# Attention of a fused graph block: values as weights in column groups instead of probabilities as weights

## The reference, cut to what matters

```
h = relu(layernorm(x))
q, k, v = split(h @ W_qkv)              # 4 heads of 32 features
s = q k^T / sqrt(32) + (adj == 0 ? -inf : 0)
x = x + softmax(s) v                    # the attention; the change is in this line
h = relu(layernorm(x))
h = relu(adj (h Wg0 + bg0));  h = relu(adj (h Wg1 + bg1))
for p in 1..4:                          # LSTMs over windows of p tokens
    h at the last token of each window = LSTM_p(window)
x = x + h
```

## Time and profile before

| | us |
|---|---|
| median of 3 runs | 554.71 (551.59 to 556.43) |
| the profiled execution | 551.66 |
| its span in the trace | 549.9 |
| PE busy | 503.4 (92%) |
| PE weight loads busy | 434.2 (79%) |
| DVE busy | 427.7 (78%) |
| ACT busy | 352.6 (64%) |
| POOL busy | 170.3 (31%) |
| mean granted clock of TensorE | 0.973 of full speed |

### The profile page before, as it was taken

The page is one execution under the profiler, slowest core; times in us unless marked ns, Lnnn a source line. Parts: engine busy times, 40 slices in busy tenths (PEclk is TensorE's granted clock), DMA queues, the critical chain, the costliest instruction groups (busy, mean ns, idle before and its releaser), DMA issues.

```text
span 549.9 us, 10009 instructions
## 1 busy us (share of the span) xinstructions
PE 503.4 (92%) x3464; PEld 434.2 (79%) x3464; DVE 427.7 (78%) x918; ACT 352.6 (64%) x573; POOL 170.3 (31%) x179
## 2 busy tenths in 40 slices
PE   3788999999999999999979999999999999999653
PEld 3577888888888888888867778889999888888533
DVE  3866787778877788776783788888888888788896
ACT  2445866668666686767757777777766577656241
POOL 2434424454344543541110012111121212233473
PEclk9999999999999999999998999999999999999975
DMA  7323000000000000000000000000000000000134
GB/s 216 102 81 92 2 2 1 2 0 0 0 0 0 0 0 0 0 0 1 2 1 0 2 0 1 1 0 2 1 1 1 2 0 1 0 1 20 58 95 134
DMA packets 18778, 11.29 MB, mean 21 GB/s; under 512 B 662, under 2 KB 17724, under 8 KB 18748
## 3 DMA queue, kind: packets, MB, share of 16 engines
q1 hardware_dynamic: 17052, 10.03, 6.3%
q10 hardware_dynamic: 1696, 0.87, 0.6%
HBM read 6.70 MB, written 4.19 MB: 20 GB/s over the span
## 4 chain that ended last, share of the span: by engine, by line
PE 62%; DVE 20%; ACT 8%; issue 6%; DMA 2%; POOL 1%; DVEq 0%; ACTq 0%; SPq 0%; POOLq 0%
PE ps L900 19%; PE ps L838 10%; PE ps L747 7%; PE ps L758 6%; DVE arena L1220 4%; DVE S_hi L1214 3%; PE ps L851 3%; DVE arena L1201 3%; PE ps L779 3%; PE ps L795 3%; PE ps L856 2%; ACT arena L587 2%; PE ps L942 2%; DVE arena L1191 2%; PE ps L769 2%
## 5 line engine op out<-in xcount | busy, mean ns | idle before, releaser
L601 ACT ACTIVATE arena<-ps,bias 128x512 f32<-128x512 f32 (+1 forms) x207 | 120.8, 626 | 38.3 <-PE ps L900 36.8
L565 ACT ACTIVATE arena<-ps 128x512 f32<-128x512 f32 (+1 forms) x112 | 85.5, 790 | 50.0 <-PE ps L758 42.3
L545 POOL TENSOR_TENSOR arena<-arena 128x512 f32<-128x512 f32 (+1 forms) x36 | 44.1, 1225 | 168.1 <-ACT arena L601 168.1
L900 PE MATMUL ps<-H_hi,W_hi 128*128 128x512 f32 (+2 forms) x207 | 76.0, 367 | 6.5 <-DVE S_lo L1216 5.1
L900 PE MATMUL ps<-H_lo,W_hi 128*128 128x512 f32 (+2 forms) x207 | 75.2, 363 | 0.0
L900 PE MATMUL ps<-H_hi,W_lo 128*128 128x512 f32 (+2 forms) x207 | 75.0, 362 | 0.0
L838 PEld LDWEIGHTS ps<-arena 128*128 128x128 f32 x512 | 64.1, 191 | 12.6 <-issue 8.4
L747 PE MATMUL ps<-ident,arena 128*128 128x128 f32 x384 | 54.6, 291 | 17.7 <-DVE arena L1220 7.8
L504 POOL TENSOR_TENSOR veps<-mv,eps 128x4 f32<-128x4 f32 x32 | 11.7, 365 | 187.0 <-DVE mv L1070 187.0
L838 PE MATMUL ps<-arena 128*128 128x33 f32 x512 | 63.5, 269 | 3.5 <-ACT arena L565 2.1
L747 PEld LDWEIGHTS ps<-ident,arena 128*128 128x128 f32 x384 | 46.1, 150 | 21.1 <-issue 9.3
(11 more groups left out here) (106 smaller groups left out, 1021.0 us busy)
## 6 DMA issues: line engine op xcount, KB each, us to landing
X<-in_x_dram SPq DMA_DIRECT2D x16, 256.0 KB, 2.8
out_dram<-X SPq DMA_DIRECT2D x14, 256.0 KB, 2.3
out_dram<-X ACTq DMA_DIRECT2D x2, 256.0 KB, 3.1
arena<-in_L_gnn_W_dram ACTq DMA_DIRECT2D x1, 128.0 KB, 3.0
wg<-in_L_gnn_Wg_dram ACTq DMA_DIRECT2D x2, 64.0 KB, 2.3
bg_rows<-in_L_gnn_bg_dram SPq DMA_DIRECT2D x6, 0.5 KB
wv<-in_L_gnn_W_dram ACTq DMA_DIRECT2D x1, 64.0 KB, 3.2
adj_sb<-in_adj_dram SPq DMA_DIRECT2D x1, 64.0 KB, 3.3
```

What stands on the lines that cost most here:

```text
L545: g_.tensor_tensor(ig[:, it.buf, 0:w], sig_i[:, it.buf, 0:w], tanh_g[:, it.buf, 0:w], ALU.mult)\
L565: a_.activation(to, psum, func).then_inc(ready, 1)
L601: a_.activation(to[:, it.buf, 0:w], ps[:, 4 * it.par + j, 0:w], func, bias=bias[:, col:col + 1])\
L900: l = mm(o, wt, v, start=m == 0, stop=m == len(terms) - 1)
```

## The change

The roles in the attention product are exchanged. The values (128 tokens x 32 features of one batch and head) become the weights, and the transposed probabilities (128 columns) move. Each head writes 32 partitions of the output, at partition 32h, so the four heads lie on four groups of 32 columns of the array. The output of a group is thus transposed: features on partitions, tokens on columns. The row sums come from four more products, with a 128x32 matrix of ones as weights and the 512 columns of each head moving; they stand in bank 5 beside the output in bank 4, repeated on the 32 partitions of the head, so that the division is elementwise. DVE takes the reciprocal of 128x512 sums and multiplies; PE transposes the quotient back into bank 5 (`attended`, four 128x128 transposes), and DVE adds it to `X` from there in the next iteration (`add_attention`, with the moments behind it).

The halves of the attention are gone: one `attend`, behind all masks, and one `over_sums`. PE's order in the iteration changes with it: K is projected behind `graph_mix`, `transpose_prob` half 1 stands behind `graph_linear_1`, `attended` stands between `scores` and the second `graph_mix`. DVE's `normalize` moves ahead of `shift` half 1. ACT's `hn2` and `u1T` move ahead of hT and gate 0. The memset of ones in `v_sb` on POOL goes.

```diff
-            def attend(s, half):
...
-                    for h in (2 * half, 2 * half + 1):
-                        o = b * 2 + h % 2
-                        l = mm(psO[:, half, o * (HD + 1):(o + 1) * (HD + 1)], probT[:, h, b * N:(b + 1) * N],
-                               v_sb[:, 1 - s.par, b, h, :], start=True, stop=True)
+            def attend(s):
+                pe.wait_ge(probT_ready, s.k * 2)
+                for h in range(HEADS):
+                    l = mm(psSum[h * HD:(h + 1) * HD, :], ones_f[:, 0:HD], probT[:, h, :], start=True, stop=True)
+                l.then_inc(att_sums, 1)
+                for b in range(GB):
+                    at_ = slice(b * N, (b + 1) * N)
+                    for h in range(HEADS):
+                        l = mm(psO[h * HD:(h + 1) * HD, at_], v_sb[:, 1 - s.par, b, h, :], probT[:, h, at_],
+                               start=True, stop=True)
+                l.then_inc(att_done, 1)
+
+            def attended(s):
+                pe.wait_ge(att_read, s.k)
+                transposed(psSum, batches(att)).then_inc(attT_done, 1)
...  (PE's iteration)
                 first_gate(s, 0, 0)
-                if s.mid:
-                    if s.front:
-                        pe.wait_ge(q_ready, k + 1)
-                    interleave([], attend(s, 0))
-                if s.front:
-                    if s.next1:
-                        pe.wait_ge(hT_hi_ready, k + 2)
-                    pe.wait_ge(att_read, 2 * k - 2)
-                    interleave([], project(s, psK, D, k_done))
                 pe.wait_ge(hn2_ready, k - 1)
...
                 interleave([], graph_mix(hn2, u1_done))
-                if s.mid:
-                    transpose_prob(s, 1)
+                if s.front:
+                    if s.next1:
+                        pe.wait_ge(hT_hi_ready, k + 2)
+                    pe.wait_ge(x2_ready, k - 1)
+                    interleave([], project(s, psK, D, k_done))
                 pe.wait_ge(u1T_ready, k - 1)
...
                 graph_linear_1().then_inc(z1_done, 1)
+                if s.mid:
+                    transpose_prob(s, 1)
                 first_gate(s, 1, 2)
...
+                    put_mask((2, 3))
+                    pe.wait_ge(q_ready, k + 1)
                     pe.wait_ge(k_ready, k + 1)
-                    masks = [lambda h=h: put_mask((h,)) for h in (2, 3)]
-                interleave(attend(s, 1), masks)
+                attend(s)
                 if s.front:
                     scores()
+                attended(s)
                 pe.wait_ge(h1_ready, k - 1)
...  (DVE)
-            def over_sums(s, half):
-                dve.wait_ge(att_done, s.k * 2 - 1 + half)
-                v_.reciprocal(rec4[:, half], o4[:, half, :, :, HD]).then_inc(rec_ready, 1)
...
+            def over_sums(s):
+                dve.wait_ge(att_sums, s.k)
+                v_.reciprocal(rec, psSum).then_inc(rec_ready, 1)
+                dve.wait_ge(rec_ready, s.k)
+                dve.wait_ge(att_done, s.k)
...
+                v_.tensor_tensor(att, psO, rec, ALU.mult).then_inc(att_read, 1)
+
+            def add_attention(k):
+                dve.wait_ge(attT_done, k - 1)
+                xg = X[:, ds(k * GB - 2 * GB, GB), :]
+                v_.tensor_tensor(xg, xg, psSum.rearrange("p (b d) -> p b d", b=GB), ALU.add).then_inc(x2_ready, 1)
+                dve.wait_ge(x2_ready, k - 1)
+                moments(1, k - 2, stats2, var2)
...  (DVE's iteration)
                 if s.back:
-                    dve.wait_ge(x2_ready, 2 * k - 2)
-                    moments(1, k - 2, stats2, var2)
+                    add_attention(k)
...
                 if s.finish:
                     output_lo(k - 3)
+                if s.back:
+                    normalize(1, k - 2, xn2, rstd2, xn2_ready)
                 if s.mid:
                     shift(s, 1)
...
-                if s.back:
-                    normalize(1, k - 2, xn2, rstd2, xn2_ready)
...
-                if s.mid:
-                    over_sums(s, 0)
...
                 if s.mid:
-                    over_sums(s, 1)
+                    over_sums(s)
...  (ACT's iteration)
+                read(hn2, hn2, xn2_ready, k - 1, hn2_ready, ACT.Relu)
                 if s.next1:
                     read_hT(psX[s.back], k + 2, 1 - s.par)
+                read(u1T[:], psA, u1_done, k - 1, u1T_ready)
                 if s.finish:
...
                     first_gate(k - 3, 0, act_i, 0, 0.5)
-                read(hn2, hn2, xn2_ready, k - 1, hn2_ready, ACT.Relu)
                 if s.mid:
                     exp(s, 1)
...
-                read(u1T[:], psA, u1_done, k - 1, u1T_ready)
```

More of the change, by code:

```diff
@@ L254, in gnn_block @@
         qT, kT, att = take(GT), take(GT), take(GT)
-        v_sb = take(V).rearrange("p (s b h d) -> p s b h d", s=2, b=GB, h=HEADS)
+        v_sb = take(2 * GT).rearrange("p (s b h d) -> p s b h d", s=2, b=GB, h=HEADS)
         prob = take(HEADS * GT)
@@ L258, in gnn_block @@
         probT = take(HEADS * GT).rearrange("p (h n) -> p h n", h=HEADS)
+        rec = take(GT)
         at[0] = attention_end = 16 * GT
@@ L296, in gnn_block @@
         psX = {True: psK, False: psB}
-        psO = ps[:, 4:6, :]
+        psO, psSum = ps[:, 4, :], ps[:, 5, :]
         def psW(m):
@@ L353, in gnn_block @@
         att_done = sem("att_done")
+        att_sums = sem("att_sums")
         rec_ready = sem("rec_ready")
         att_read = sem("att_read")
+        attT_done = sem("attT_done")
         x2_ready = sem("x2_ready")
@@ L492, in _ @@
             g_.memset(eps[:], LN_EPS)
-            g_.memset(ident[:], 0.0)
-            g_.memset(v_sb[:, :, :, :, HD:HD + 1], 1.0).then_inc(pool_chain, 1)
+            g_.memset(ident[:], 0.0).then_inc(pool_chain, 1)
             pool.wait_ge(pool_chain, 1)
@@ L654, in read_v @@
                 if s.back:
-                    act.wait_ge(att_done, 2 * s.k - 2)
-                a_.activation(v_sb[:, s.par, :, :, 0:HD], psA.rearrange("p (b h d) -> p b h d", b=GB, h=HEADS),
+                    act.wait_ge(att_done, s.k - 1)
+                a_.activation(v_sb[:, s.par, :, :, :], psA.rearrange("p (b h d) -> p b h d", b=GB, h=HEADS),
                               ACT.Copy).then_inc(v_ready, 1)
@@ L978, in fill @@
                     pe.wait_ge(w_lo_done, 2)
+                if s.mid:
+                    pe.wait_ge(probT_ready, k * 2 - 1)
                 put_mask((0, 1))
@@ L982, in fill @@
                     pe.wait_ge(k_ready, k + 1)
-                    interleave(attend(s, 1), [lambda h=h: put_mask((h,)) for h in (2, 3)])
+                    put_mask((2, 3))
+                    attend(s)
                 else:
@@ L1001, in iteration @@
                         pe.wait_ge(w_lo_done, 2 * MAX_SKIP)
-                    pe.wait_ge(att_read, 2 * k - 3)
+                    pe.wait_ge(att_read, k - 1)
                     interleave([], project(s, psQ, 0, q_done))
@@ L1036, in iteration @@
                 graph_linear_1().then_inc(z1_done, 1)
+                if s.mid:
+                    transpose_prob(s, 1)
                 first_gate(s, 1, 2)
-                masks = []
                 if s.front:
+                    pe.wait_ge(probT_ready, k * 2 - 1)
                     put_mask((0, 1))
                     pe.wait_ge(probT_ready, k * 2)
+                    put_mask((2, 3))
+                    pe.wait_ge(q_ready, k + 1)
                     pe.wait_ge(k_ready, k + 1)
-                    masks = [lambda h=h: put_mask((h,)) for h in (2, 3)]
-                interleave(attend(s, 1), masks)
+                attend(s)
                 if s.front:
                     scores()
+                attended(s)
                 pe.wait_ge(h1_ready, k - 1)
@@ L1143, in shift @@
                     .then_inc(shifted, 1)
-            def over_sums(s, half):
-                dve.wait_ge(att_done, s.k * 2 - 1 + half)
-                v_.reciprocal(rec4[:, half], o4[:, half, :, :, HD]).then_inc(rec_ready, 1)
[L1149 to L1156, removed]
+            def over_sums(s):
[3 more added lines that the diff above has]
+                dve.wait_ge(att_done, s.k)
+                if not s.prep:
+                    dve.wait_ge(attT_done, s.k - 1)
+                v_.tensor_tensor(att, psO, rec, ALU.mult).then_inc(att_read, 1)
[5 more added lines that the diff above has]
+                moments(1, k - 2, stats2, var2)
             def first_cell_part(g):
```

16 lines of the change are left out of this document (2 added, 14 removed).

## The result

The changed kernel takes 606.25 us in the median of four runs (604.89 to 607.11), the kernel before 555.57 beside it: a ratio of 1.092, 95% interval 1.086 to 1.098. Slower was forecast, at 592 and within 572 to 620. The profiled executions took 604.89 and 551.66 us, 53.2 apart.

A forecast was written before the change was run, and what follows sets the result against it. PE bounded the kernel at 17.28 us a period; DVE's reciprocal would make it 19.55, + 2.3. 16 x 2.3 = 37 us on 551.66 gives 588.5; that execution lies 3.05 under the median, so 592, range 572 to 620.

The forecast's parts named there:

- The reciprocal decides: DVE's 128x512 reciprocal takes 3.2 us, with no cover beyond attend and scores; period from 17.28 to 19.55 us.
- a quick one (0.73): Rival: DVE's reciprocal takes 0.73 us; PE's period 17.55 and 559 us, or 539 with waits covered; 9%.
- a dearer one (4.5): Rival: DVE's reciprocal takes 4.5 us, 1.3 us more idle stretch each period, 612 us; 8%.
- The estimate of 4.4 us: DVE's reciprocal if the skill's repeat count of 8 meant eight cycles an element; about 19 us more on the total.
- The idle stretch ahead of `attended`: PE ends attend and scores at 17.55 and idles 2.0 us until DVE's product is done at 19.55.
- The rival of serial column groups: Rival: PE's column groups run one behind the other, hiding the reciprocal; + 5.3 us a group, 640 us; 10%.
- the rule on weight loads: Skill's rule: a weight load overlaps products in flight only when row groups differ; by it PE's attention would be serial.
- about 1.2 us: PE's attention by the skill's 2.38x for three column tiles; it would leave the sum as it is.
- The loop: From PE's attended through DVE, POOL, ACT and PE back to the next attended: a period of 19.55 us.
- The waits of 0.6 and 0.4: PE waits 0.6 us at graph_mix, and 0.4 us ahead of the second transposition of the probabilities.
- TensorE's clock: Rival: the clock falls behind the 2.0 us of idle in every period, 24 us, 616 us; 13%.
- PE's saving of 1.0 us: PE's attention takes 2.6 us a group instead of 3.6; PE alone would gain 1.0, or 16 us.

The follow-up runs named there:

- The copy: Changed kernel with a tensor copy of 128x512 in place of the reciprocal, the division left out: 554.73 us, ratio 1.003.
- the half: Changed kernel with the reciprocal on 256 of the 512 columns and a copy on the other 256: 572.60 us, ratio 1.034.
- Moving the transposes: Changed kernel with PE's transposes of the quotient put behind the second graph_mix and gate 2: 596.71 us, ratio 1.076.
- keeping PE busy: Changed kernel with eight 512-column products, result unread, between scores and the wait for the quotient: 590.06 us, ratio 1.065.
- head by head: Changed kernel with the values' products issued head by head instead of batch by batch: 591.85 us, ratio 1.069.

## Why the prediction was right, and where it fell short

- **The reciprocal decides.** Right. 3.2 us were drawn from eight elements, 3.35 measured. The copy shows that it makes the whole loss (1.003 instead of 1.092), with the clock's falls behind its wait in it, and the half shows the price by the column. The rivals of a quick one (0.73) and a dearer one (4.5) fall. The estimate of 4.4 us, from eight cycles an element, falls too.
- **The idle stretch ahead of `attended`.** Right: 2.0 forecast, 2.36 measured, since the products in column groups were quicker than taken: 0.88 and 0.99 instead of 1.1 and 1.1. The rival of serial column groups falls. So does the rule on weight loads that the prediction quoted from the Trainium skill ("TensorE: Matmul & The Clock Gate", Part 3): 32 instructions that share their row groups and alternate over four column groups, each with a weight load of its own, took 31 ns each, less than half of the 74 on one group. The same 32 instructions are 2.37 / 0.99 = 2.4 times quicker on four groups in turn than one group after the other, which is close to the 2.38x that the same part states for three column tiles; the "about 1.2 us" that the prediction took from it stands there without its working.
- **The loop.** Right to 0.05 us: 19.55 forecast, 19.50 measured. That it is so close is luck in part: the reciprocal took 0.15 longer than forecast and began, from PE's transposes, at 238.76 - 223.42 = 15.34 instead of 15.5, and the two cancel. Moving the transposes (19.4 where the clock held) shows that it runs over DVE. The waits of 0.6 and 0.4 came as 0.54 and less than 0.3.
- **TensorE's clock.** This is the term of the sum that was mis-sized. The forecast took it at nothing ("clock at 1.00 in the steady part" was among its signs), with a rival that priced a fall in every period at 1.5 us a group, and falls in some periods as "inside the range". They came in about 12 of 16 at 1.34 us, 16 us in all; keeping PE busy took just that off. Nor did a fall come in every period, as the rival had it, and which periods it picks stays open. 592 and 16 make 608, against 606.25. The mechanism and its price stood there, but the likeliest number went by the case without it, although the one fall in the earlier trace rows had come behind a shorter wait (1.39 us) than the 2.0 forecast here. Those rows spoke for taking it.
- **PE's saving of 1.0 us.** Its size was right (16.22 busy against 16.93 is 0.7, and the 1.0 held 0.24 of wait beside), and that it is worth nothing was shown: with a cheap operation for the reciprocal the period is 17.37. The forecast's price for that case, 17.55 and 559, was near (554.73). Where it goes is shown only in part: 0.34 us are `normalize`'s wait for POOL; the rest lies by the trace on the path over graph linear 2 and `output_lo`, which no run shortened.

## What to carry to other kernels

A reciprocal on DVE is to be priced by the column (6.25 ns here, six times a plain operation), so a division belongs where the sums have the fewest columns, and making it elementwise to save a broadcast is dear. Before an engine's work is cut, follow the loop that would bound next: one engine's wait can be moved (0.44 instead of 2.36) without the period changing. And an idle stretch of some 2 us on PE can cost twice, once as itself and once as the lower clock behind it: here it did in 9 of 13 steady periods.

## What the runs showed of the hardware

- The reciprocal: 128x8 in 0.21 us, 128x16 in 0.25, 128x256 in 1.75, 128x512 in 3.35. A copy of 128x512 out of PSUM takes 0.68.
- Column groups of 32 overlap: four in turn 31 ns an instruction (128 moving columns, float32), one alone 74. Eight instructions of 512 columns with 32 weight columns, in pairs on each group, take 0.88 us.
- A reciprocal of 128x512 costs 96 us where it is added in the old order (648.35 against 551.95) and 51 where it stands for a copy in the new one (606.25 against 554.73), with the clock at its lower level for 10.2 us of each period in the first.
- The clock fell in 9 of 13 steady periods with one wait of PE of 2.2 to 2.4 us, and in 9 of 13 with three of 0.44, 0.69 and 1.34; it held in all with one of 0.8 to 1.1 in that place (head by head, and the half reciprocal).
- Work that nobody needs made two kernels faster, by 16 and by 47 us.
